# Turning a batch's attention output back in two row tiles and two ring banks instead of one

## What is computed

```python
q = split_heads(query @ Wq.T + bq)          # 16 heads of 16
k = split_heads(key @ Wk.T + bk)
v = split_heads(value @ Wv.T + bv)
scores = einsum('bhqd,bhkd->bhqk', q, k) / sqrt(16) + relative_bias
attn = softmax(where(key_padding_mask, scores, -inf), axis=-1)
out = einsum('bhqk,bhkd->bhqd', attn, v)
out = out.transpose(0, 2, 1, 3).reshape(4, 512, 256)
x = x + tanh(g) * (out @ Wo.T + bo)
```

## Time and profile before

| | us |
|---|---|
| median of 3 runs | 945.96 (940.16 to 947.39) |
| the profiled execution, device time | 947.89 |
| its span, first to last instruction | 946.1 |
| PE, DVE, ACT, POOL busy in the span | 896.5, 564.1, 452.4, 461.6 |
| turned outputs in the span | 32, of 4 transposes each |

### The profile page before, as it was taken

How to read it: one execution, slowest core, us unless ns; L and a number is a source line. 1 busy time by engine, 2 the same in 40 slices (tenths; PEclk the granted TensorE clock), 3 DMA queues, 4 the chain that set the end, 5 groups by cost and what they waited for, 6 DMA issues and landing times. The chain is left out here.

```text
span 946.1 us, 20996 instructions
## 1 busy us (share of the span) xinstructions
PE 896.5 (95%) x7733; PEld 554.6 (59%) x7734; DVE 564.1 (60%) x1659; ACT 452.4 (48%) x645; POOL 461.6 (49%) x648
## 2 busy tenths in 40 slices
PE   6869999998989999999999999997999899999998
PEld 2456555554557554456555555574556677777765
DVE  4537999997938434367999999746522222222226
ACT  2416878776754233336888788833111123222221
POOL 2006888887857700007888888731265022222224
PEclk9985999999999999996999999999999999999999
DMA  8664454544123433444242524032822012222116
GB/s 276 239 219 180 139 178 145 172 148 124 36 70 130 141 112 95 123 138 115 68 126 68 125 73 124 16 94 106 284 85 97 11 57 68 62 61 67 58 59 239
DMA packets 69988, 111.82 MB, mean 118 GB/s; under 512 B 17190, under 2 KB 41194, under 8 KB 67722
## 3 DMA queue, kind: packets, MB, share of 16 engines
q1 hardware_dynamic: 62266, 91.26, 31.6%
q10 hardware_dynamic: 4224, 9.96, 3.5%
q0 software_dynamic: 3408, 9.38, 2.8%
HBM read 76.99 MB, written 33.58 MB: 117 GB/s over the span
## 5 line engine op out<-in xcount | busy, mean ns | idle before, releaser
L736 ACT ACTIVATE pT<-ps 128x1024 f32<-128x1024 f32 x224 | 220.0, 1027 | 81.7 <-PE ps L606 81.6
L786 POOL TENSOR_SCALAR s<-s,nmax 128x512 f32<-128x512 f32 x218 | 149.2, 698 | 179.5 <-DVE nmax L677 176.4
L786 POOL TENSOR_SCALAR xT<-xT,nmax 128x512 f32<-128x512 f32 x224 | 153.9, 699 | 52.7 <-DVE nmax L677 52.7
L677 DVE CUSTOM_DVE_ANT_0 xT<-ps,bias 128x512 f32<-128x512 f32 x240 | 156.4, 688 | 20.1 <-PE ps L592 11.6
L677 DVE CUSTOM_DVE_ANT_0 s<-ps,bias 128x512 f32<-128x512 f32 x224 | 146.0, 688 | 18.7 <-PE ps L592 12.9
L592 PE MATMUL ps<-ks,qs 49*128 49x512 f32 (+1 forms) x512 | 140.7, 509 | 12.7 <-DMA qs<-qk_scratch 8.4
L624 PE MATMUL ps<-pT,vq 128*32 128x512 f32 x1024 | 137.0, 612 | 3.1
L592 PEld LDWEIGHTS ps<-ks,qs 49*128 49x128 f32 (+1 forms) x512 | 57.5, 198 | 122.5 <-DVE nmax L677 87.7
L1673 POOL DMA_INDIRECT slots_out<-y,id x39 | 37.8, 970 | 140.4 <-DVE y L2009 137.1
L1757 PE MATMUL ps<-gu,xgT 128*128 x312 | 98.8, 460 | 0.7 <-ACT xgT L1841 0.7
L606 PEld LDWEIGHTS ps<-ident,xT 64*128 64x128 f32 x2048 | 78.7, 144 | 7.8 <-issue 3.4
(11 more groups left out here) (202 smaller groups left out, 1209.7 us busy)
## 6 DMA issues: line engine op xcount, KB each, us to landing
bias<-in_bias SPq DMA_DIRECT2D x13, 1024.0 KB, 6.9
qs<-qk_scratch SPq DMA_DIRECT2D x180, 64.0 KB, 2.3
ks<-qk_scratch SPq DMA_DIRECT2D x62, 128.0 KB, 3.0
gu<-in_gate_up SPq DMA_DIRECT2D x8, 704.0 KB, 8.8
slots_in<-zeros SPq DMA_DIRECT2D x4, 1280.0 KB, 6.3
xg<-slots_in SPq DMA_DIRECT2D x39, 130.0 KB
qk_scratch<-parts ACTq DMA_DIRECT2D x8, 512.0 KB
qk_scratch<-parts SPq DMA_DIRECT2D x8, 512.0 KB
```

The source lines that it names most:

```text
L677: nc.vector.tensor_tensor_reduce(at.s[n % 4][:, k, :], sb.ps[:, ring_bank(tile_place[u]), :], at.bias[bias % BIAS_SLOTS][:, k, :], -1.0, 3 ...
L736: nc.scalar.activation(at.pT[:, slot(m // HG, m % HG), 2 * half:2 * half + 2, :], sb.ps[:, 2 + 2 * half:4 + 2 * half, :], ACT.Exp).then_in ...
L786: nc.gpsimd.tensor_scalar(s, s, -1.0, at.nmax[:, n % 4, k:k + 1], ALU.mult, ALU.add).then_inc(pool_less_max, 1)
```

## The change

The turned output takes two ring places, one for each row tile: `ring_out` appends two entries. `turn_out` waits for the entries three places back of both, and then issues eight transposes of 64 rows, alternating between the row tiles, each half into its own bank. DVE reads the two halves with two reciprocals of 8 sums and two multiplications of 128 elements, and each half signals for itself; `rsum` is laid out by halves.

```diff
     def ring_out():
 
         out_place.append(len(ring))
-        ring.append((out_done, len(out_place) + 1))
+        for r in range(2):
+            ring.append((out_done, 2 * len(out_place) + r))
...
             def turn_out(hg, b):
                 pe.wait_ge(out_kept, hg * B + b + 2)
                 place = out_place[hg * B + b]
-                pe.wait_ge(*ring[place - 3])
+                for r in range(2):
+                    pe.wait_ge(*ring[place + r - 3])
                 for qt in range(QT):
-                    last = nc.tensor.transpose(sb.ps[:, ring_bank(place), qt * P:(qt + 1) * P], at.oT[:, qt * P:(qt + 1) * P],
-                                               sb.ident[:, :])
+                    for r in range(2):
+                        rows = slice(r * HP, (r + 1) * HP)
+                        last = nc.tensor.transpose(sb.ps[:, ring_bank(place + r), qt * HP:(qt + 1) * HP],
+                                                   at.oT[rows, qt * P:(qt + 1) * P], sb.ident[rows, rows])
                 last.then_inc(out_turned, 1)
...
             def invert_sums(hg, b):
-                dve.wait_ge(out_turned, hg * B + b + 2)
-                dve.wait_ge(out_done, hg * B + b + 1)
-                nc.vector.reciprocal(at.rsum[:, :, :], turned_out(hg, b)[:, :, :, DH]).then_inc(sums_ready, 1)
+                k = hg * B + b
+                dve.wait_ge(out_turned, k + 2)
+                dve.wait_ge(out_done, 2 * k + 1)
+                for r in range(2):
+                    nc.vector.reciprocal(at.rsum[:, r, :, :], turned_out(hg, b, r)[:, :, :, DH]).then_inc(sums_ready, 1)
 
             def normalise(hg, b):
-                dve.wait_ge(sums_ready, hg * B + b + 1)
...
+                for r in range(2):
+                    dve.wait_ge(sums_ready, 2 * (hg * B + b) + r + 1)
+                    nc.vector.tensor_tensor(
+                        dst[:, hg, r, :, :].rearrange("p t (j d) -> p t j d", j=HG // 2),
+                        turned_out(hg, b, r)[:, :, :, 0:DH],
+                        at.rsum[:, r, :, :].unsqueeze(3).to_broadcast([P, QT, HG // 2, DH]),
+                        ALU.mult).then_inc(out_done, 1)
```

More of the change, by code:

```diff
@@ L679, in add_bias, with turned_out @@
                     -1.0, 3.0e38, ALU.add, ALU.min, at.nmax[:, n % 4, k:k + 1]).then_inc(biased, 1)
-            def turned_out(hg, b):
-                return sb.ps[:, ring_bank(out_place[hg * B + b]), :].rearrange("p (t j w) -> p t j w", t=QT, j=HG)
+            def turned_out(hg, b, r):
+                return sb.ps[:, ring_bank(out_place[hg * B + b] + r), 0:QT * HP].rearrange(
+                    "p (t j w) -> p t j w", t=QT, j=HG // 2)
             def invert_sums(hg, b):
-                dve.wait_ge(out_turned, hg * B + b + 2)
-                dve.wait_ge(out_done, hg * B + b + 1)
-                nc.vector.reciprocal(at.rsum[:, :, :], turned_out(hg, b)[:, :, :, DH]).then_inc(sums_ready, 1)
-            def normalise(hg, b):
-                dve.wait_ge(sums_ready, hg * B + b + 1)
[L692 to L696, removed]
+                k = hg * B + b
[3 more added lines that the diff above has]
+                    nc.vector.reciprocal(at.rsum[:, r, :, :], turned_out(hg, b, r)[:, :, :, DH]).then_inc(sums_ready, 1)
+            def normalise(hg, b):
+                dst = sb.tok[:, b * QT:(b + 1) * QT, 0:D].rearrange("p t (g r f) -> p g r t f", g=GROUPS, r=2)
+                for r in range(2):
[5 more added lines that the diff above has]
+                        ALU.mult).then_inc(out_done, 1)
             for u in range(AHEAD):
@@ L2130, in build @@
                 at.nmax = buf("nmax", [P, 4, QT], F32)
-                at.rsum = buf("rsum", [P, QT, HG], F32)
+                at.rsum = buf("rsum", [P, 2, QT, HG // 2], F32)
                 s01 = buf("s", [P, 2, QT, S], F32)
```

## The result

| | before | changed |
|---|---|---|
| median, us | 943.99 (4 runs, 940.16 to 947.39) | 961.73 (4 runs, 957.60 to 967.92) |
| ratio, 95% interval | | 1.0179 (1.0141 to 1.0217) |
| profiled execution, its span | 947.89, 946.1 | 967.92, 966.2 |
| one step in the attention | 11.78 | 12.40 |

A forecast was written before the change was run, and what follows sets the result against it. PE bounds the attention step (busy 11.67 of 11.78 us). Later turned outputs, odd steps and ends sum to 16.4 us, with tile d's 1.1 to 17.5: profiled execution 965.4, median 963.5 us, 1.9% slower; range 953 to 971.

The forecast's parts named there:

- (1): Turned output on PE: eight row-tile transposes take 0.25 us, two tile changes fewer; unobstructed, 0.42 us won each step.
- (2): Second ring place: the turned output waits for tile a, starts 1.37 behind S, T at 1.62, 0.61 us later.
- (3): DVE's two more instructions per turned output, 0.96 us in place of 0.67, lie in its wait for PE, costing nothing.
- (4): Scores of tile d wait for the first half's multiplication: about even, taken as 0.04 us a step.
- Rival C: DVE's halves are slow: tile d and V wait 0.28 us a step, not 0.04; 970 us; chance 0.15.
- (5): Odd steps and layer ends: bias-wait step loses 0.31 us, one other 0.45; about 0.1 won in each layer.
- B: Loss is taken up elsewhere, in PE slack: 954 us if half, 946 if all; chance 0.08.
- D: PE's clock falls after stalls: 14 us more, 978 us, if every third step lost 1.5; chance 0.06.
- A: Bank is no obstacle, transposes start right behind S: 0.42 us a step, 11.8 us won, 934 us; chance 0.07.

## Why the prediction was right, step by step

(1) Eight transposes take 0.27 us from TO to T (503.51 to 503.78), forecast 0.25; the empty stretch on PEld ahead of T is gone. The one ahead of TO is not all due to the change of tile: in the run with the row tiles alone, where no tile changes and nothing waits, 0.17 of its 0.24 is left (479.28), and TO starts 0.38 behind S, where I had 0.34. T to the next S has become 0.98 in place of 1.02, which I had not counted.

(2) The wait for tile a is the loss, as the run with the wait alone shows: TO at 1.38 (forecast 1.37), T at 1.65 (1.62), each of the regular steps 0.62 longer (0.61). The 0.15 us from a's accumulator to TO, chosen from the row of the same instruction, is what the changed kernel shows, 503.36 to 503.51; with half of the pieces ahead of the wait it is 0.06 for the other half.

(3) DVE's instructions cost nothing, as forecast; the run with six more of them behind the multiplications shows how much room there is. Two readings in that part were slips without effect: b is done at 1.83 and not by 1.75 (the reciprocal's row starts before the accumulator's ends), and four instructions of the old length, ending at 3.19, would have cost c 0.02 and not nothing.

(4) The wait of tile d was put at 0.04 a step and is nil: the first multiplication ends early enough. The run with work ahead of the multiplications shows that the wait is there and bites once it ends later. Rival C had the right mechanism and the wrong lengths.

(5) The odd step cannot be compared, since the bias wait came in another step; it lost more than the 0.31 forecast: it is 4.62 us longer than a regular step, where it was 3.75, with a mean clock of 0.80 in place of 0.89.

The sum of 17.5 us stands against 17.7 between the medians and 17.5 within the attention of the two profiled executions. The cause and the size of a regular step are right; that the sums agree so closely is in part luck. The 1.1 us put on tile d did not come, and the first layer's 13 distances grew by 8.70 us, where 11 at 0.61 with 0.31 and 0.45 for the two odd ones make 7.5. Nor do the runs tell the total to better than 13 to 20 us.

Rivals: B falls, since no part of the wait was taken up elsewhere. D falls for regular steps (clock 1.00 in the window of one step). A was rightly given little, but its price was wrong: with the bank no obstacle I had 0.42 a step and 11.8 us to win, and the versions that keep one place win 0.13 to 0.14. The next wait of the same ring, d for b at 1.89 to 1.90, stands right behind the one that I took away, and I had not followed it.

## What to carry to other kernels

Where engines hand tiles through a short ring of banks, one more place for one item moves every wait behind it one item nearer; with three banks the writer then needs the reader to be done with what it has only just been given. Price such a change by walking the ring: for each writer, which tile frees its place, when that tile's reader can have finished at the earliest, and what would be waited for next if this wait went. If splitting an operation needs a second buffer only to keep its halves from meeting, setting the halves apart in time in the same buffer can keep the gain.

## What the runs showed of the hardware

- TO's first transpose starts 0.15 us behind the end of the accumulator row it waits for (503.36 to 503.51), where three waits stand ahead of it. With half of the pieces ahead of the wait, the fifth, which has one wait, starts 0.06 behind (485.96 to 486.01), as a score matmul does (478.27 to 478.33). The granted clock was 1.00 in these steps; that the number of waits makes the difference is not shown.
- Transposes of one row tile follow each other every 0.06 us and those of two row tiles, taken by turns, every 0.03; where T's pieces of the other row tile are next in the queue they start between the former (486.12, with TO's last pieces at 486.13 and later).
- Reciprocals of 8 sums last 0.16 to 0.21 us each, but six of them, back to back, push what follows by 0.39: some 0.07 each.
